# New places for the pre-core and post-core stages in a software pipeline written out by hand

## The chip, the cores and the metric

The kernel runs on one core of a Trainium2 chip. The metric is the device time of one execution in microseconds (us), the median of several runs. A core has five engines that work beside each other, each from a queue of its own and strictly in order: PE (TensorE, matrix products into PSUM banks), DVE (VectorE), ACT (ScalarE), POOL (GpSimd) and SP (SyncE, which only issues DMAs here). They meet through semaphores.

## The reference

There are 16 samples of 512 tokens with 128 channels. Each goes through four residual blocks, each behind a layer normalisation:

```
x = x + block_a(_layernorm(x))     # Mamba block: conv, 16 states, scan over 512 tokens, feed-forward
x = x + experts(_layernorm(x))     # e1: 8 heads, product keys 32 x 32, 8192 experts
x = x + block_b(_layernorm(x))     # gated scan with 16 states, one row each
x = x + experts(_layernorm(x))     # e2: the same expert weights
```

Block a computes for each of 256 inner channels and 16 states `h = exp(delta*A)*h + delta*u*B`, and `y = sum over the states of h*C`. The expert layer forms, for each token and head, two sets of 32 similarities, takes the best key of each, and fetches one of 8192 pairs of rows (`w_down`, `w_up`) by the two keys. The token's result is `gelu(x . w_down) * relu(score) * w_up`, summed over the eight heads.

## The kernel before, in words

The 128 partitions hold channels in the scans and tokens elsewhere; a sample has 4 tiles of 128 tokens. The work of a sample has three phases. The *core* is the scan of block a: for state n, ACT makes the decay `dA` (L1027), PE broadcasts B and C (L759, L768), DVE feeds (L1338), scans (L1354, 128x1024) and reads out (`hp` times C, L1364); for states 1, 3, ..., 13 POOL does the read-out (L1483) from a copy of C that ACT makes (`c_row`, L1044). PE adds the products of all states up in `ysum` (L784), and DVE gates the sum (L1450). *Pre-core* is what comes ahead of it (norm, convolution, silu, the step sizes), *post-core* what follows: the rest of block a, e1, block b, e2.

`run_pipeline` goes through iterations -1 to 19. Iteration i holds the core of sample i, the pre-core of sample i + 1 and the post-core of samples i - 1 to i - 4, so up to six samples are in flight. Iterations 5 to 14 are a hardware loop with two iterations in its body. An iteration is cut into 64 slots, four for each state of the core. Each engine's program goes through the slots in order and issues the stages that `SLOTS` puts there: a post-core slot s means slot s % 64 of iteration (sample + 1 + s // 64). From iteration 15 on, `LAST_SLOTS` replaces the places where it has an entry. A slot is no time: it only sets the order in which an engine meets its stages. What a stage waits for is the same wherever it stands.

An expert layer has these stages, with two halves of two token tiles or four tiles each. PE `sim` (L680) makes the similarities of a tile in one of two PSUM banks; DVE `top` takes the maxima (L1233) and a mask of where they are (L1240). For two tiles, PE `flip` transposes the masks (L691), ACT `flip` copies them (L987), PE `code` turns them to codes (L703), and DVE `index` reads the codes (`bits`, L1249) and makes row numbers (L1258). POOL `fetch` issues eight stages of four indirect gathers (L1468) for the four tiles; its first stage of a half waits for the index and for the previous sample's `sum` to have read the row buffer, and later ones for the landing of the stage two before. DVE `dot` multiplies the rows with the token (L1267, eight for a tile), ACT takes the gelu (L994), DVE `weigh` makes coefficients (L1274), ACT `scale` multiplies the rows (L1006), PE `sum` adds them (L713, L717) and ACT `out` takes the result out (L999).

PE's two shared banks are guarded: `claim` waits until the consumer of the bank's previous content has read it, `fill` notes the next. ACT has to load a table when it changes between groups of functions; `needs` (L934) issues the load where the next function in order asks for another table than the last:

```
if table[0] != name:
    act.preload_act_table_set(name)
    table[0] = name
```

So the number of loads follows from the order on ACT alone. SP issues the loads of x for the residual (`sp_xres`) and the stores of y (`sp_store`).

Of the kernel before, what the change touches and what calls it, by code (L numbers as in the profile page):

```python
# [58 lines left out]
    "pe_turn_x": (PRE, (10,)),  # L59
    "pe_conv": (PRE, (13, 18, 24, 26)),  # L60
    "pe_xproj": (PRE, (35,)),
    "pe_rest": (PRE, (38, 42)),
    "pe_dt": (PRE, (43, 44)),
    "pe_skip": (CORE, (58,)),
    "pe_out": (POST, (0,)),
    "pe_ff1": (POST, (0,)),
    "pe_ff2": (POST, (7,)),
    "pe_ln_a": (POST, (10,)),
    "pe_turn_e1": (POST, (27,)),
# [4 lines left out]
    "pe_turn_b": (POST, (118,)),  # L74
    "pe_xp": (POST, (120,)),
    "pe_gate": (POST, (122,)),
    "pe_y": (POST, (124,)),
    "pe_z": (POST, (143,)),
    "pe_ln_c": (POST, (147,)),
# [6 lines left out]
    "act_rms_x": (PRE, (3,)),  # L86
    "act_keep_x": (PRE, (10,)),
    "act_norm_x": (PRE, (4,)),
    "act_turn_x": (PRE, (6,)),
    "act_conv": (PRE, (14, 19, 24, 28)),  # L90
    "act_silu": (PRE, (30, 63)),
    "act_dbl": (PRE, (34,)),
    "act_soft": (PRE, (42, 47)),
    "act_split": (PRE, (37, 41)),
    "act_exp": (PRE, (55,)),
    "act_ln": (PRE, (56,)),
    "act_out": (POST, (1,)),
    "act_gelu": (POST, (2,)),
    "act_rstd_a": (POST, (5,)),
    "act_rstd_e1": (POST, (17,)),  # L100
    "act_norm_e1": (POST, (24,)),
    "act_turn_e1": (POST, (29,)),
    "act_flip_e1": (POST, (42, 51)),
    "act_gelu_e1": (POST, (64, 81)),
    "act_scale_e1": (POST, (70, 72, 86, 91)),
    "act_out_e1": (POST, (91, 96)),
    "act_rstd_b": (POST, (108,)),
    "act_norm_b": (POST, (120,)),
    "act_turn_b": (POST, (121,)),
    "act_xp": (POST, (125,)),  # L110
    "act_gate": (POST, (125,)),
    "act_tanh": (POST, (128,)),
    "act_rstd_c": (POST, (144,)),
    "act_rstd_e2": (POST, (171,)),
    "act_norm_e2": (POST, (174,)),
    "act_turn_e2": (POST, (177,)),
# [1452 lines left out]
```

## Time and profile before

| what | value |
|---|---|
| time, median of three runs | 1968.15 us (1953.9 to 1971.99) |
| profiled execution | 1957.38 us, span 1955.6 us |
| mean granted clock of PE | 0.938 |
| busy: DVE | 1661.3 us (85%), 4204 instructions |
| busy: PE | 1608.4 us (82%), 6097 matmuls |
| busy: ACT | 1537.7 us (79%), 3276 instructions |
| busy: POOL | 1358.5 us (69%), 1209 instructions |

The shares are means over stages with different limits. The first samples fill the pipeline; the gatings of samples 1 to 14 follow each other in 92 to 109 us; the gating of sample 15, at 1716.20, ends the last core iteration; and from there to 1955.6 the post-core of the last samples runs with no core beside it. A view by windows keeps these stretches apart.

### The profile page before, as it was taken

What the parts mean: (1) busy time and instruction counts of PE and PEld (TensorE: products, weight loads), DVE (VectorE), ACT (ScalarE), POOL (GpSimd) and SP (SyncE); (2) the same over time, 40 slices, a digit from 0 to 9 for tenths busy, and PEclk for the clock granted to TensorE, in tenths of its full rate; (3) what the DMA queues carried; (4) which work ended last, traced back from release to release, by engine and by line L of the source; (5) the groups of instructions that cost most, each with busy time, mean ns of one, the idle gap of its engine ahead of it and who ended that gap; (6) DMA issues with size and microseconds to landing.
All of it is one profiled execution on the core that took longest, in us unless ns stands there. A gap on an engine that the chain in (4) does not pass through costs nothing. (4 is left out here: it accounts for less than half of the span.)

```text
span 1955.6 us, 24773 instructions
## 1 busy us (share of the span) xinstructions
PE 1608.4 (82%) x6097; PEld 887.0 (45%) x6186; DVE 1661.3 (85%) x4204; ACT 1537.7 (79%) x3276; POOL 1358.5 (69%) x1209
## 2 busy tenths in 40 slices
PE   5788788879898988898898989898989986766653
PEld 2333344445454545454454545454545443444332
DVE  3889989899998999999999999999999998844431
ACT  5666778789897979898898989898998975465543
POOL 0234647488877787787778788777778777776665
PEclk8899899999999999999999999999999997997776
DMA  2000212023323223232323232322323232233232
GB/s 60 11 11 27 71 29 70 27 79 86 88 83 93 81 79 96 76 98 81 93 84 90 84 99 79 92 87 67 103 81 95 83 85 83 76 102 98 87 95 83
DMA packets 79901, 151.06 MB, mean 77 GB/s; under 512 B 20584, under 2 KB 46592, under 8 KB 79680
## 3 DMA queue, kind: packets, MB, share of 16 engines
q0 software_dynamic: 49152, 134.28, 24.0%
q1 hardware_dynamic: 29344, 14.65, 2.7%
q8 instruction: 61, 1.00, 0.2%
q14 instruction: 96, 0.79, 0.1%
q10 hardware_dynamic: 1248, 0.34, 0.1%
HBM read 145.01 MB, written 4.19 MB: 76 GB/s over the span
## 5 line engine op out<-in xcount | busy, mean ns | idle before, releaser
L1468 POOL DMA_INDIRECT rows<-in_experts,index x1024 | 981.9, 959 | 357.2 <-issue 288.8
L1354 DVE TENSOR_TENSOR_SCAN hp<-dA,fed_ps 128x1024 f32<-128x1024 f32 x256 | 583.7, 2280 | 7.7 <-issue 2.9
L784 PE MATMUL ysum<-hp,ident 128*128 128x512 f32 x1024 | 487.6, 621 | 4.0 <-DVE hp L1364 3.4
L1483 POOL TENSOR_TENSOR hp<-hp,c_row 128x1024 f32<-128x1024 f32 x112 | 264.8, 2364 | 219.7 <-ACT c_row L1044 178.0
L1027 ACT ACTIVATE dA<-delta,decay 128x511 f32<-128x511 f32 x512 | 334.7, 711 | 17.2 <-issue 15.4
L1338 DVE TENSOR_TENSOR fed_ps<-du,b_ps 128x1024 f32<-128x1024 f32 x256 | 313.7, 1225 | 39.2 <-PE b_ps L759 23.5
L1006 ACT ACTIVATE rows<-rows,coef 128x128 f32<-128x128 f32 x1024 | 311.1, 390 | 13.1 <-DVE coef L1274 13.1
L784 PEld LDWEIGHTS ysum<-hp,ident 128*128 128x128 f32 x1024 | 206.7, 202 | 219.4 <-issue 201.7
L934 ACT ACT_TABLE_LOAD x218 | 279.7, 1283 | 8.8 <-PEq L544 5.0
L717 PE MATMUL bank<-rows,ident 128*128 128x256 f32 x1024 | 251.2, 402 | 32.5 <-ACT rows L1006 32.5
L1267 DVE CUSTOM_DVE_ANT_0 rows<-rows,xn 128x128 f32<-128x128 f32 x1024 | 240.9, 298 | 39.5 <-DMA rows<-in_experts,index 39.1
L717 PEld LDWEIGHTS bank<-rows,ident 128*128 128x128 f32 x1024 | 208.2, 204 | 67.3 <-ACT rows L1006 35.1
L680 PE MATMUL bank<-w_sim,xnT 128*128 128x512 f32 x256 | 151.4, 676 | 46.9 <-DVE mask L1240 32.8
L1364 DVE TENSOR_TENSOR hp<-hp,c_ps 128x1024 f32<-128x1024 f32 x144 | 174.4, 1211 | 13.0 <-remote 12.5
L1233 DVE TENSOR_REDUCE top<-bank 128x16 f32<-128x512 f32 x128 | 86.9, 679 | 43.7 <-PE bank L680 42.7
L810 PE MATMUL bank<-xrT,w_taps 128*128 128x512 f32 x256 | 117.3, 601 | 2.4 <-ACT ucs L1118 1.5
L759 PE MATMUL b_ps<-split,pick 128*128 128x512 bf16 x243 | 97.2, 400 | 21.9 <-DVE fed_ps L1338 11.7
L768 PE MATMUL c_ps<-split,pick 128*128 128x512 bf16 x182 | 73.3, 403 | 38.3 <-DVE hp L1364 30.0
L1240 DVE TENSOR_TENSOR mask<-bank,top 128x512 bf16<-128x512 f32 x128 | 88.6, 692 | 13.0
L999 ACT ACTIVATE x<-bank 128x256 f32<-128x256 f32 x64 | 24.2, 379 | 90.1 <-PE bank L717 89.5
L680 PEld LDWEIGHTS bank<-w_sim,xnT 128*128 128x128 f32 x256 | 43.6, 201 | 113.1 <-DVE mask L1240 63.8
L987 ACT ACTIVATE flip<-bank 128x1024 bf16<-128x1024 bf16 x64 | 65.0, 1015 | 36.3 <-PE bank L691 34.9
(182 smaller groups left out, 2195.4 us busy)
## 6 DMA issues: line engine op xcount, KB each, us to landing
rows<-in_experts,index POOLq DMA_INDIRECT x1024, 2.7
x_in<-in_x SPq DMA_DIRECT2D x16, 256.0 KB, 4.1
x_res<-in_x SPq DMA_DIRECT2D x16, 256.0 KB, 4.7
y<-x SPq DMA_DIRECT2D x16, 256.0 KB, 2.7
rows<-in_taps SPq DMA_DIRECT2D x1, 512.0 KB
rows<-in_wq_t SPq DMA_DIRECT2D x1, 512.0 KB, 5.2
rows<-in_in_proj_t ACTq DMA_DIRECT2D x1, 256.0 KB
rows<-in_key_t SPq DMA_DIRECT2D x1, 128.0 KB, 5.2
```

Source lines behind the costliest of these rows:

```text
L680: nc.tensor.matmul(bank[k][:], e.xnT[:, t * P:(t + 1) * P], w_sim[:], start=True, stop=True).then_inc(e.sim, 1)
L717: mm = nc.tensor.matmul(total, ident[:], e.rows[:, tiles, h, P:2 * P], start=False, stop=(h == HEADS - 1), skip_group_check=True)
L784: mm = nc.tensor.matmul(ysum[:, j, :], ident[:], hp[:, BUFFER[k], j, :], start=(k == SUM_ORDER[0]), stop=(k == SUM_ORDER[-1]))
L934: act.preload_act_table_set(name)
L1006: op = nc.scalar.activation(row, row, ACT.Copy, scale=e.coef[:, t, h:h + 1])
L1027: op = nc.scalar.activation(dA[:, n % NDA, j, 1:T], delta[q][:, j, 1:T], ACT.Exp, scale=decay[:, j, n:n + 1])
L1267: op = nc.vector.tensor_tensor_reduce(row, row, e.xn[r][:, t, :], 1.0, 0.0, ALU.mult, ALU.add, e.dot[:, t, h:h + 1])
L1338: nc.vector.tensor_tensor(fed_ps[:], src[:], b_ps[:].to_broadcast([P, NH, T]), ALU.mult).then_inc(fed, 1)
L1354: nc.vector.tensor_tensor_scan(flat, dA[:, n % NDA, :, :].rearrange("p a b -> p (a b)"), fed_ps[:].rearrange("p a b -> p (a b)"), 0.0, ALU ...
L1364: nc.vector.tensor_tensor(state, state, c_ps[:].to_broadcast([P, NH, T]), ALU.mult).then_inc(read_out, 1)
L1468: pool.indirect_dma_start(e.rows[:, t, h, :], None, A["experts"], bass.IndirectOffsetOnAxis(ap=e.index[:, t, h:h + 1], axis=0)).then_inc(e ...
L1483: pool.tensor_tensor(state, state, c_row[:, k % NCR, :].unsqueeze(1).to_broadcast([P, NH, T]), ALU.mult).then_inc(pool_read, 1)
```

## The change

The numbers in `SLOTS` and `LAST_SLOTS` are new; nothing else is changed. Every stage still issues the same instructions with the same waits and the same buffers. The order in which an engine meets its stages changes on PE, ACT, DVE and POOL; on SP the order is the same. Of the roughly 150 changed entries these are the ones of which the text speaks, and some around them:

```diff
 SLOTS = {
...
-    "pe_sim_e1": (POST, (35, 39, 44, 45)),
-    "pe_flip_e1": (POST, (42, 49)),
-    "pe_code_e1": (POST, (43, 49)),
+    "pe_sim_e1": (POST, (33, 38, 43, 48)),
+    "pe_flip_e1": (POST, (40, 49)),
+    "pe_code_e1": (POST, (42, 52)),
...
-    "pe_turn_e2": (POST, (175,)),
-    "pe_sim_e2": (POST, (176, 178, 185, 186)),
-    "pe_flip_e2": (POST, (180, 192)),
-    "pe_code_e2": (POST, (184, 193)),
-    "pe_sum_e2": (POST, (236, 251)),
+    "pe_turn_e2": (POST, (176,)),
+    "pe_sim_e2": (POST, (179, 180, 183, 185)),
+    "pe_flip_e2": (POST, (181, 190)),
+    "pe_code_e2": (POST, (182, 197)),
+    "pe_sum_e2": (POST, (240, 251)),
...
-    "act_silu": (PRE, (30, 63)),
+    "act_silu": (PRE, (30, 59)),
...
-    "act_flip_e2": (POST, (184, 192)),
-    "act_gelu_e2": (POST, (221, 239)),
-    "act_scale_e2": (POST, (224, 228, 241, 252)),
+    "act_flip_e2": (POST, (187, 192)),
+    "act_gelu_e2": (POST, (220, 246)),
+    "act_scale_e2": (POST, (228, 237, 252, 253)),
...
-    "dve_top_e1": (POST, (38, 40, 45, 48)),
-    "dve_index_e1": (POST, (42, 53)),
-    "dve_dot_e1": (POST, (54, 63, 75, 78)),
-    "dve_weigh_e1": (POST, (66, 82)),
+    "dve_top_e1": (POST, (36, 39, 47, 48)),
+    "dve_index_e1": (POST, (40, 52)),
+    "dve_dot_e1": (POST, (60, 62, 67, 76)),
+    "dve_weigh_e1": (POST, (68, 81)),
...
-    "dve_top_e2": (POST, (177, 180, 184, 185)),
-    "dve_index_e2": (POST, (183, 198)),
-    "dve_dot_e2": (POST, (210, 219, 228, 237)),
-    "dve_weigh_e2": (POST, (224, 239)),
+    "dve_top_e2": (POST, (178, 180, 183, 184)),
+    "dve_index_e2": (POST, (181, 198)),
+    "dve_dot_e2": (POST, (212, 220, 228, 242)),
+    "dve_weigh_e2": (POST, (224, 245)),
-    "pool_delta": (PRE, (59,)),
-    "pool_x1": (POST, (4,)),
-    "pool_x3": (POST, (120,)),
-    "pool_fetch_e1": (POST, (39, 42, 44, 53, 61, 62, 66, 70)),
-    "pool_fetch_e2": (POST, (192, 201, 205, 209, 214, 219, 223, 228)),
-    "sp_xres": (POST, (14,)),
-    "sp_store": (POST, (234,)),
+    "pool_delta": (PRE, (55,)),
+    "pool_x1": (POST, (5,)),
+    "pool_x3": (POST, (121,)),
+    "pool_fetch_e1": (POST, (39, 44, 46, 53, 55, 56, 57, 58)),
+    "pool_fetch_e2": (POST, (187, 198, 207, 211, 218, 220, 225, 228)),
+    "sp_xres": (POST, (35,)),
+    "sp_store": (POST, (251,)),
 LAST_SLOTS = {
...
-    "pe_sim_e2": (POST, (164, 171, 178, 180)),
+    "pe_sim_e2": (POST, (171, 171, 184, 190)),
...
-    "pe_sum_e2": (POST, (240, 244)),
+    "pe_sum_e2": (POST, (243, 253)),
...
-    "act_gelu_e2": (POST, (221, 243)),
-    "act_scale_e2": (POST, (232, 235, 243, 244)),
+    "act_gelu_e2": (POST, (227, 242)),
+    "act_scale_e2": (POST, (231, 235, 247, 250)),
...
-    "dve_top_e2": (POST, (168, 175, 179, 180)),
-    "dve_index_e2": (POST, (175, 203)),
-    "dve_dot_e2": (POST, (218, 220, 242, 243)),
+    "dve_top_e2": (POST, (171, 174, 190, 191)),
+    "dve_index_e2": (POST, (177, 196)),
+    "dve_dot_e2": (POST, (212, 222, 241, 247)),
...
-    "pool_fetch_e1": (POST, (35, 37, 47, 47, 48, 49, 53, 62)),
-    "pool_fetch_e2": (POST, (176, 177, 204, 210, 212, 219, 220, 227)),
+    "pool_fetch_e1": (POST, (27, 31, 32, 40, 50, 52, 55, 56)),
+    "pool_fetch_e2": (POST, (187, 196, 200, 207, 210, 212, 218, 238)),
```

On DVE a loop iteration had, from slot 48 on:

```
scan 12, top_e1.3, feed 13, top_e2.0, mul 12, scan 13, top_e2.1, feed 14, index_e1.1, dot_e1.0,
index_e2.0, scan 14, top_e2.2, feed 15, top_e2.3, mul 14, scan 15, mul 15, scan_b, dot_e1.1
```

and has with the change:

```
scan 12, top_e1.3, feed 13, mul 12, dot_e2.3, top_e2.0, scan 13, top_e2.1, index_e1.1, feed 14,
index_e2.0, weigh_e2.1, top_e2.2, scan 14, top_e2.3, feed 15, mul 14, scan 15, dot_e1.0, mul 15,
dot_e1.1, scan_b
```

where `mul` is the read-out and the number behind the point is the tile or half. On PE, ahead of the flips of e2's first half, stood `sum_e2.0, sim_e1.3, turn_e2, sums of 12, sim_e2.0, flip_e1.1, code_e1.1, sim_e2.1, sums of 13`, and now `turn_e2, sim_e1.3, sum_e2.0, flip_e1.1, sim_e2.0, sums of 13, sim_e2.1, code_e1.1`.

## Rows read from the trace of the kernel before

**Rows 1.** Windows: length, busy PE, PEld, DVE, ACT, POOL (count), PEclk, DMA, GB/s.

```profile
950.70:1057.50 106.80, 94.66 (x381) 53.00 (x388) 101.75 (x262) 97.76 (x207) 84.82 (x76) 1.00 0.31 87
...
1591.50:1717.40 125.90, 93.12 (x351) 52.23 (x354) 107.46 (x248) 74.19 (x181) 93.54 (x88) 0.88 0.29 85
...
1870.00:1955.60 85.60, 36.85 (x149) 24.74 (x147) 24.54 (x166) 33.75 (x96) 47.69 (x51) 0.72 0.30 86
```

**Rows 2.** Waits of DVE, 629 to 1483 us (eight iterations): total, times, longest.

```profile
DVE hp L1364 <- remote: 9.1, 8, 1.1
DVE top L1233 <- PE bank L680: 4.2, 4, 1.1
...
DVE fed_ps L1338 <- issue: 0.2, 1, 0.2
```

**Rows 3.** Timeline of DVE in iteration 10: start, duration, instruction.

```profile
1139.52 0.69 DVE L1240 TENSOR_TENSOR mask<-bank,top 128x512 bf16<-128x512 f32 x1
1140.12 1.22 DVE L1338 TENSOR_TENSOR fed_ps<-du,b_ps 128x1024 f32<-128x1024 f32 x1
1141.25 0.18 DVE L1249 TENSOR_SCALAR bits<-bank 128x32 int32<-128x32 int32 x1
...
1141.96 0.29 DVE L1267 CUSTOM_DVE_ANT_0 rows<-rows,xn 128x128 f32<-128x128 f32 x1
...
1143.66 0.19 DVE L1249 TENSOR_SCALAR bits<-bank 128x32 int32<-128x32 int32 x1
...
1144.20 2.29 DVE L1354 TENSOR_TENSOR_SCAN hp<-dA,fed_ps 128x1024 f32<-128x1024 f32 x1
```

**Rows 4.** Timeline, last samples: a mask and the bits that wait for it.

```profile
1888.39 0.69 DVE L1240 TENSOR_TENSOR mask<-bank,top 128x512 bf16<-128x512 f32 x1
...
1891.83 0.19 DVE L1249 TENSOR_SCALAR bits<-bank 128x32 int32<-128x32 int32 x1 [2.75 <-PE bank L703]
```

**Rows 5.** Timeline near 1750 us: a mask and the next maximum.

```profile
1749.17 0.69 DVE L1240 TENSOR_TENSOR mask<-bank,top 128x512 bf16<-128x512 f32 x1
...
1751.07 0.69 DVE L1233 TENSOR_REDUCE top<-bank 128x16 f32<-128x512 f32 x1 [1.22 <-PE bank L680]
```

**Rows 6.** Timeline of PE in iteration 10.

```profile
1137.39 3.60 PE L784 MATMUL ysum<-hp,ident 128*128 128x512 f32 x8
```

**Rows 7.** Groups by line: count, busy, mean ns, idle before.

```profile
L934 ACT ACT_TABLE_LOAD x218 | 279.7, 1283 | 8.8 <-PEq L544 5.0
```

**Rows 8.** Timeline of ACT about a table load.

```profile
1829.97 1.28 ACT L934 ACT_TABLE_LOAD   x1
1831.27 0.30 ACT L939 ACTIVATE lnB<-mvB,eps 128x4 f32<-128x4 f32 x1
```

**Rows 9.** Timeline of DVE, last core iteration: first scan and gating.

```profile
1591.46 2.27 DVE L1354 TENSOR_TENSOR_SCAN hp<-dA,fed_ps 128x1024 f32<-128x1024 f32 x1
...
1716.20 1.23 DVE L1450 TENSOR_TENSOR ucs<-ysum,ucs 128x1024 f32<-128x1024 f32 x1 [2.60 <-PE ysum L784]
```

**Rows 10.** Waits of ACT, 1591 to 1717 us.

```profile
ACT act L994 <- DVE dot L1267: 17.9, 4, 13.7
```

**Rows 11.** Timeline of POOL, 1717 to 1940 us: the gathers that waited, and the last.

```profile
1756.76 0.94 POOL L1468 DMA_INDIRECT rows<-in_experts,index  x1 [4.99 <-DVE index L1258]
...
1782.26 0.94 POOL L1468 DMA_INDIRECT rows<-in_experts,index  x1 [5.80 <-issue]
...
1850.74 0.94 POOL L1468 DMA_INDIRECT rows<-in_experts,index  x1 [7.47 <-PE bank L717]
...
1899.14 0.94 POOL L1468 DMA_INDIRECT rows<-in_experts,index  x1 [6.33 <-PE bank L717]
...
1938.00 0.95 POOL L1468 DMA_INDIRECT rows<-in_experts,index  x1 [0.30 <-issue]
```

**Rows 12.** Timeline of SP at the end.

```profile
1952.90 0.37 SPq L640 DMA_DIRECT2D y<-x  x1
```

**Rows 13.** Waits of DVE, 45 to 215 us.

```profile
DVE fed_ps L1338 <- PE b_ps L759: 9.4, 5, 3.7
```

More of the change, by code:

```diff
@@ L58 @@
 SLOTS = {
[L59 to L63, printed above, removed]
+    "pe_turn_x": (PRE, (8,)),
+    "pe_conv": (PRE, (10, 17, 24, 25)),
+    "pe_xproj": (PRE, (33,)),
+    "pe_rest": (PRE, (37, 40)),
+    "pe_dt": (PRE, (41, 43)),
     "pe_skip": (CORE, (58,)),
     "pe_out": (POST, (0,)),
-    "pe_ff1": (POST, (0,)),
+    "pe_ff1": (POST, (3,)),
     "pe_ff2": (POST, (7,)),
-    "pe_ln_a": (POST, (10,)),
@@ L97 @@
+    "act_conv": (PRE, (13, 21, 25, 28)),
+    "act_silu": (PRE, (30, 59)),
+    "act_dbl": (PRE, (36,)),
+    "act_soft": (PRE, (39, 41)),
+    "act_split": (PRE, (37, 38)),
+    "act_exp": (PRE, (48,)),
+    "act_ln": (PRE, (50,)),
     "act_out": (POST, (1,)),
-    "act_gelu": (POST, (2,)),
-    "act_rstd_a": (POST, (5,)),
+    "act_gelu": (POST, (1,)),
+    "act_rstd_a": (POST, (4,)),
     "act_rstd_e1": (POST, (17,)),
-    "act_norm_e1": (POST, (24,)),
-    "act_turn_e1": (POST, (29,)),
-    "act_flip_e1": (POST, (42, 51)),
@@ L104 @@
[L104 to L109, printed above, removed]
+    "act_norm_e1": (POST, (23,)),
+    "act_turn_e1": (POST, (28,)),
+    "act_flip_e1": (POST, (39, 54)),
+    "act_gelu_e1": (POST, (64, 79)),
+    "act_scale_e1": (POST, (71, 71, 86, 89)),
+    "act_out_e1": (POST, (90, 98)),
+    "act_rstd_b": (POST, (101,)),
+    "act_norm_b": (POST, (119,)),
@@ L170 @@
-    "pe_sum_e2": (POST, (240, 244)),
+    "pe_out": (POST, (0,)),
+    "pe_ff1": (POST, (0,)),
+    "pe_ff2": (POST, (8,)),
+    "pe_ln_a": (POST, (15,)),
+    "pe_turn_e1": (POST, (26,)),
+    "pe_sim_e1": (POST, (26, 28, 33, 33)),
+    "pe_flip_e1": (POST, (30, 40)),
+    "pe_code_e1": (POST, (31, 40)),
+    "pe_sum_e1": (POST, (81, 85)),
+    "pe_turn_b": (POST, (108,)),
+    "pe_xp": (POST, (112,)),
+    "pe_gate": (POST, (112,)),
+    "pe_y": (POST, (117,)),
+    "pe_z": (POST, (132,)),
+    "pe_ln_c": (POST, (136,)),
@@ L171 @@
+    "pe_turn_e2": (POST, (160,)),
+    "pe_sim_e2": (POST, (171, 171, 184, 190)),
+    "pe_flip_e2": (POST, (174, 191)),
+    "pe_code_e2": (POST, (174, 199)),
+    "pe_sum_e2": (POST, (243, 253)),
     "act_out": (POST, (3,)),
     "act_gelu": (POST, (3,)),
[L173 to L174 removed]
+    "act_rstd_a": (POST, (9,)),
+    "act_rstd_e1": (POST, (19,)),
     "act_norm_e1": (POST, (24,)),
[L176 to L177 removed]
@@ L205 @@
[L205 to L215 removed]
+    "act_turn_e1": (POST, (25,)),
@@ new lines @@
+    "act_flip_e1": (POST, (30, 42)),
+    "act_gelu_e1": (POST, (51, 76)),
+    "act_scale_e1": (POST, (72, 76, 77, 77)),
+    "act_out_e1": (POST, (83, 88)),
+    "act_rstd_b": (POST, (90,)),
+    "act_norm_b": (POST, (99,)),
+    "act_turn_b": (POST, (111,)),
+    "act_xp": (POST, (112,)),
+    "act_gate": (POST, (112,)),
+    "act_tanh": (POST, (126,)),
+    "act_rstd_c": (POST, (136,)),
+    "act_rstd_e2": (POST, (140,)),
+    "act_norm_e2": (POST, (150,)),
+    "act_turn_e2": (POST, (159,)),
@@ new lines @@
+    "act_flip_e2": (POST, (173, 194)),
+    "act_gelu_e2": (POST, (227, 242)),
+    "act_scale_e2": (POST, (231, 235, 247, 250)),
+    "act_out_e2": (POST, (242, 252)),
+    "dve_x1": (POST, (15,)),
+    "dve_stats_e1": (POST, (16,)),
+    "dve_shift_e1": (POST, (20,)),
+    "dve_top_e1": (POST, (26, 29, 32, 34)),
+    "dve_index_e1": (POST, (31, 44)),
+    "dve_dot_e1": (POST, (41, 53, 67, 71)),
+    "dve_weigh_e1": (POST, (66, 76)),
+    "dve_stats_b": (POST, (92,)),
+    "dve_shift_b": (POST, (93,)),
```

107 lines of the change are left out of this document (29 added, 78 removed).

## The prediction

> **What bounds the kernel now.** I read the windows by stage first, because the kernel has three different regimes [rows 1]. In the loop, from one gating of the scan's sum to the next, DVE is busy 101.75 of 106.80 us, ACT 97.8, PE 94.7, POOL 84.8, at the full granted clock: DVE is the bound. In the last core iteration DVE is busy 107.5 of 125.9 us, and in the last stretch 24.5 of 85.6 while the clock is down to 0.72. The reader should then see, in the table of waits over eight loop iterations, how little DVE has left to win [rows 2]: 9.1 us for the read-out of state 15, 4.2 us for the similarities of the key search, and so on down to 0.2 us. Its eight kinds of wait come to 22.6 us in eight iterations, 2.8 us each. A new order cannot shorten DVE's work; in the loop it can win at most these 2.8 us an iteration, while what it can lose has no such lid. For the last core iteration and what follows, the timelines of DVE and POOL are read, where one sees who waits for whom; they stand with their parts below.
>
> **The change, part by part.** No instruction is added or removed, and no wait or buffer. What changes is the order in which each engine's queue holds its stages. I wrote out both orders for each engine and iteration and asked, for each wait, which work now stands between the producer and the consumer.
>
> *Loop, the e2 search (loss).* Before, DVE has between the second mask of e2 (ends 1140.21) and the first index of e2 (1143.66) a feed of 1.22 us, an index of 0.7 us and a dot stage of 1.7 us, so 3.5 us of cover [rows 3]. Behind a mask the chain PE flip, ACT flip, PE code takes 2.75 us until DVE can read its bits; this row is at a reduced clock, so at full clock I take 2.4 as the lower end [rows 4]. Afterwards the dot stage has left this place; feed and index are all the cover there is, 1.75 us from the mask's end to the index's (1140.21 to 1141.96). The stall is 2.4 to 2.75 less 1.75, so 0.65 to 1.0. On ACT two table loads and the second silu now stand ahead of this flip too; they may add half a microsecond or hide behind the PE's stages. I take 0.9, bounds 0.4 to 1.5.
>
> *Loop, third similarity of e2 (loss).* From a mask to the next maximum on the same bank the trace shows 1.22 us of waiting through PE's matmul pair [rows 5]. Before, a scan of 2.29 us stands there and hides it [rows 3]; afterwards only a weigh stage does, one short instruction. Because the two banks alternate, part may hide: I take 1.1, bounds 0.7 to 1.3.
>
> *Loop, two smaller losses.* The first index of e1 has one scan (2.29) ahead of it in place of feed, read-out and statistics: against the same chain 0.3, bounds 0 to 0.6. The second similarity of e2 is now behind the summing of state 12 and 13 on PE, which takes 3.60 us [rows 6], while DVE does a dot stage, a maximum with its mask and a scan: 0.5, bounds 0 to 1. The loss comes to 0.9 + 1.1 + 0.3 + 0.5 = 2.8 us an iteration, bounds 1.1 to 4.4.
>
> *Loop, gains.* The first dot stage of e1 (1.7 us) moves to between scan 15 and the read-out of state 15, where DVE waits 9.1/8 = 1.14 us [rows 2]; that wait is covered whole. The fourth similarity of e1 gets a scan for cover, which should end the similarity waits, 4.2/8 = 0.53 [rows 2]; smaller ones give 0.2. Gain 1.9, and it is nearly the lid. Net +0.95 us an iteration, bounds -0.3 to +2.3. The full post-core work stands in iterations 3 to 14, so twelve times: +11 us, bounds -4 to +28.
>
> *Loop, other engines.* Counted from ACT's order, the table loads fall from the 218 of the trace to 205, one less in each loop iteration. At 1.283 us that frees 16.7 us of ACT [rows 7], but ACT is not the bound, so I cost it at nothing; its cover is ACT's own 9 us of slack in each iteration [rows 1]. POOL now issues the last two e1 stages and the first e2 stage at the end of an iteration and spills 13 to 15 us into the next; the first POOL read-out then comes some 3 to 5 us later by the same hand walk, still before PE sums its state, and POOL has 22 us of slack [rows 1]. The loading of the residual moves 21 slots later and the store 17; the queue of SP holds them in the same order and both land long before their readers, so nothing.
>
> At one place a row and a rule part. When ACT changes its table, the load takes 1.28 us and the next ACTIVATE starts 0.02 us after it [rows 8]. The Trainium skill, "ScalarE: Activation LUTs", section "What ACT_TABLE_LOAD costs", gives 1283 ns for the load and another 1380 ns for a drain, some 2.66 us a switch. By that the thirteen saved loads would be worth 35 us of ACT, still off DVE's path; the trace agrees on the load and shows no drain here.
>
> *Last core iteration (gain).* From its first scan (1591.46) to its gating (1716.20) it takes 125 us [rows 9], some 18 longer than a loop iteration; ACT waits 13.7 us at once for a dot stage [rows 10], which waits for its fetched rows. POOL here does the fetches of two samples ahead of time, and the new places issue e1 of sample 14 from slot 27 in place of 35, and defer three e2 stages. Walking the order by hand with the durations of these rows puts the gating 112 to 122 us after the first scan; I take 117, so -8, bounds -13 to 0. Against it: the gating now stands behind the last two similarity stages of e2 of sample 12 and a sum of sample 11 on PE, and its wait of 2.60 us [rows 9] grows to some 8 us, which is in the 117.
>
> *Tail (gain).* After the gating POOL does little but issue row gathers, at a pitch of 0.95 + 0.30 = 1.25 us, so a stage of four is 5.0 us; it has four waits: 4.99 (for the index of sample 15), 5.80, 7.47 and 6.33 us, the last three before the first e2 stage of samples 13, 14 and 15 [rows 11]. In the new order the last e2 stage of sample 12 and the first two of sample 13 are issued among and behind e1 of sample 15: the 5.80 goes with its place. Behind the 7.47 stood six stages, 30 us, since the last fetch of e1, so the chain it waited for is 37.5 us long; now eight stages and a short addition stand there, some 41 us, and it vanishes too: -13.3. One more stage comes after the index of sample 15: +5.0. That index comes about 1.3 us later, and the last output has one gelu more ahead of it, +0.25. If the 6.33 us wait keeps its length, -7; if it ends when it did, 0. I take -4, with the upper bound at +2. From the last gather (1938.95) to the store (1952.90) 14 us pass [rows 11, 12]; that stays.
>
> *Head (unknown).* In the first iterations DVE waits 9.4 us in five waits for B's broadcast [rows 13]. Some places ahead of it become earlier, one later; no row prices that, so a few of these 9.4 us either way: -2, bounds -5 to +3.
>
> **Sum.** +11 - 8 - 4 - 2 = -3 us. The profiled execution took 1957.4 us, 10.8 under the median of the three runs: it should become 1954, and the median 1965.
>
> **Rivals.** (A) The covers suffice, faster: if PE and ACT are ahead of DVE at these places, the losses of the loop shrink to 0.2 and the gain of 1.9 stays: 12 x -1.7 = -20; with -8, -4 and -2 that is -34, so 1934. For it: PE and ACT are idle 12 and 9 us in a loop iteration, so they can be early. Against it: the chain behind a mask begins with DVE's own mask, and no idle time elsewhere shortens it.
> (B) The e2 search becomes DVE's bound, slower: PE's run of turn, sum, similarity, summing, similarity comes late as one, and each of DVE's four e2 similarities then waits. The upper end of the loop, 2.3 x 12 = +28, with nothing won in the last core iteration, gives 1996. It decides from more than 1 us of waiting ahead of the second e2 similarity in each iteration, or a gating more than 125 us after the first scan of sample 15. For it: the stages of e2 now stand back to back. Against it: the read-out wait is surely covered.
> (C) Only the order in a saturated queue changes, and every wait that goes comes back elsewhere: 1968.
> (D) The two table loads that now stand ahead of the first e2 flip each cost twice their 1.28 us, because ACT empties before a load: 2 x 1.28 more a loop iteration, 12 x 2.6 = +31, so 1996. The row with 0.02 us after a load speaks against it. It is the rule of the Trainium skill's page "ScalarE: Activation LUTs", section "What ACT_TABLE_LOAD costs".
>
> **Chances.** My forecast 0.36, (A) 0.30, (B) 0.22, (C) 0.08, (D) 0.04. One per cent, 20 us, is about what a measurement of this kernel can tell from no change, since its own three runs lie 18 us apart. Faster by over 1%: 0.30 from (A). Within: 0.36 + 0.08 = 0.44. Slower: 0.22 + 0.04 = 0.26. My forecast by itself spans 1949 to 1985 (its bounds added as squares, -16 and +20); the range reaches to (A) and to (B) and leaves out a tenth beyond either: 1930 to 1998.
>
> **What would show it.** In the changed kernel's loop: waits of the bits for PE's code of about 0.9 + 0.3 us an iteration, and of the maximum for the similarity of about 1.5; no wait of the read-out of state 15; a period near 107.7 us. 205 table loads. The gating of sample 15 near 117 us after its first scan. One wait in place of three between POOL's e2 stages in the tail, and the end some 235 us after that gating. I am wrong if the loop's period falls under 106 (A) or exceeds 109 (B, D), or if the last gating comes later than before.

## The result, and the profile after

The changed kernel takes 2008.83 us (median, 2007.79 to 2009.21) where the kernel before took 1969.47: ratio 1.0222, 95% interval 1.0179 to 1.0266. It is slower by 2.2%, where 0.2% faster was forecast, and it lies above the stated range. Its executions differ by 1.4 us; those of before by 18.

The profiled execution has a span of 2007.0 us, 51.4 more than before. Cut at the gatings, as in [rows 1, 9]:

| stretch | before, us | after, us | difference | forecast |
|---|---|---|---|---|
| start to gating of sample 2 | 311.1 | 310.9 | -0.2 | -2 |
| iterations 3 to 14 | 1279.2 | 1341.9 | +62.7 | +11 |
| last core iteration | 125.9 | 121.4 | -4.5 | -8 |
| gating of sample 15 to end | 239.4 | 232.8 | -6.6 | -4 |

So the whole error lies in the loop, whose period rose from 106.7 to 112.6 us. The windows of the changed kernel (one loop iteration, the last core iteration, the tail; columns as in [rows 1]):

```profile
1089.60:1202.30 112.70, 98.21 (x380) 56.34 (x386) 107.02 (x261) 94.41 (x204) 85.46 (x76) 0.94 0.29 83
1652.80:1774.20 121.40, 91.40 (x345) 50.67 (x349) 105.71 (x247) 68.55 (x163) 85.34 (x78) 0.90 0.27 78
1774.20:2007.00 232.80, 138.66 (x574) 90.72 (x574) 86.75 (x514) 122.33 (x332) 158.13 (x166) 0.76 0.34 98
```

The reader should see that DVE is busy 107.0 us in an iteration of the loop, for the work that took it 101.75 [rows 1]; the counts, 261 and 262, differ only by where the windows are cut. The same work has become longer. Its waits, over eight iterations as in [rows 2], grew too, but less:

```profile
DVE top L1233 <- PE bank L680: 19.1, 25, 1.3
DVE s L1367 <- ACT rr L941: 8.8, 4, 2.4
DVE bits L1249 <- PE bank L703: 5.7, 8, 0.7
DVE fed_ps L1338 <- PE b_ps L759: 1.1, 3, 0.4
```

The wait for the read-out of state 15 is gone, as forecast. Which instructions are longer is read from the groups by line, over the same eight iterations (busy, mean ns, idle before). First the kernel before:

```profile
L1267 DVE CUSTOM_DVE_ANT_0 rows<-rows,xn 128x128 f32<-128x128 f32 x512 | 114.6, 286 | 0.2
...
L1437 DVE TENSOR_TENSOR_SCAN gates<-gates 16x512 f32<-16x512 f32 x8 | 9.7, 1212 | 0.3
...
L1258 DVE TENSOR_SCALAR index<-code 128x16 uint32<-128x16 f32 x32 | 5.8, 180 | 1.1
```

and the changed kernel:

```profile
L1267 DVE CUSTOM_DVE_ANT_0 rows<-rows,xn 128x128 f32<-128x128 f32 x512 | 113.9, 285 | 0.5 <-DMA rows<-in_experts,index 0.2
...
L1258 DVE TENSOR_SCALAR index<-code 128x16 uint32<-128x16 f32 x32 | 29.5, 922 | 1.1
L1437 DVE TENSOR_TENSOR_SCAN gates<-gates 16x512 f32<-16x512 f32 x8 | 21.9, 2734 | 0.3
```

Two groups out of some thirty hold the rise: the last instruction of the index stage, +23.7 us, and the scan of block b, +12.2 us, together 4.5 us an iteration. Neither is a long instruction by itself. What POOL does at such a moment is seen when the two timelines are laid beside each other. The index stage of iteration 10 on DVE:

```profile
1102.35 0.17 DVE L1254 SCALAR_TENSOR_TENSOR code<-bits 128x16 f32<-128x16 int32 x1
1102.56 4.07 DVE L1258 TENSOR_SCALAR index<-code 128x16 uint32<-128x16 f32 x1
1106.54 2.27 DVE L1354 TENSOR_TENSOR_SCAN hp<-dA,fed_ps 128x1024 f32<-128x1024 f32 x1
```

and POOL over the same stretch:

```profile
1102.06 0.95 POOL L1468 DMA_INDIRECT rows<-in_experts,index  x1 [0.30 <-issue]
1103.03 2.35 POOL L1483 TENSOR_TENSOR hp<-hp,c_row 128x1024 f32<-128x1024 f32 x1
1105.32 1.26 POOL L1489 TENSOR_TENSOR x_res<-x_res,ln_b 128x512 f32<-128x512 f32 x1
```

An instruction of 0.17 us began under a gather, was then held through POOL's read-out of state 1 and the addition right behind it, and ended 0.05 us after that addition (1106.63 against 1106.58). POOL lost nothing: 2.35 and 1.26 us are its ordinary times. The scan of block b, on DVE in iteration 9:

```profile
1085.64 2.78 DVE L1437 TENSOR_TENSOR_SCAN gates<-gates 16x512 f32<-16x512 f32 x1
...
1088.46 1.23 DVE L1338 TENSOR_TENSOR fed_ps<-du,b_ps 128x1024 f32<-128x1024 f32 x1
```

with POOL's addition for block b under it, and behind that a gather that is itself 0.75 us longer than its 0.95:

```profile
1086.07 1.27 POOL L1494 TENSOR_TENSOR xnb<-x,beta 128x512 f32<-128x512 f32 x1
1087.50 1.70 POOL L1468 DMA_INDIRECT rows<-in_experts,index  x1 [0.16 <-issue]
```

In the kernel before, the same scan began under gathers alone in each loop iteration and took 1.21 us. I call it a meeting when a DVE instruction is lengthened in this way. Summed over the whole execution as the excess of each instruction over its group's usual time, meetings hold 17.6 us in the kernel before, all but about 1 us of it in iterations 1 to 3 and 15, and 60.4 us in the changed kernel.

The other predicted rows: 205 table loads at 1283 ns, as counted. The first index of sample 15 reached POOL 41.4 us after the gating, 0.8 us later than before, where 1.3 was forecast. Of the three later waits in the tail one went and two stayed, shorter (rows to be held against [rows 11, 12]):

```profile
1815.57 0.95 POOL L1468 DMA_INDIRECT rows<-in_experts,index  x1 [2.60 <-DVE index L1258]
...
1906.60 0.94 POOL L1468 DMA_INDIRECT rows<-in_experts,index  x1 [4.55 <-issue]
...
1950.17 0.94 POOL L1468 DMA_INDIRECT rows<-in_experts,index  x1 [2.69 <-issue]
```

### The profile page after: what moved, and what is told of

Read it like the earlier page. It is cut to its first block and busy times, and to the rows that moved or that the text cites. A ratio compares the mean times of both kernels' runs of the same rounds, so it can differ in the third digit from the quotient of the medians.

```text
span 2007.0 us, 24736 instructions
## 1 busy us (share of the span) xinstructions
PE 1645.5 (82%) x6097; PEld 919.5 (46%) x6186; DVE 1701.2 (85%) x4204; ACT 1520.9 (76%) x3263; POOL 1364.7 (68%) x1209
## 5 line engine op out<-in xcount | busy, mean ns | idle before, releaser
L1354 DVE TENSOR_TENSOR_SCAN hp<-dA,fed_ps 128x1024 f32<-128x1024 f32 x256 | 582.6, 2276 | 1.7
L1027 ACT ACTIVATE dA<-delta,decay 128x511 f32<-128x511 f32 x512 | 332.7, 711 | 23.7 <-issue 15.3
L1338 DVE TENSOR_TENSOR fed_ps<-du,b_ps 128x1024 f32<-128x1024 f32 x256 | 313.5, 1225 | 26.8 <-PE b_ps L759 16.7
L934 ACT ACT_TABLE_LOAD x205 | 263.0, 1283 | 8.6 <-PEq L544 5.0
L1267 DVE CUSTOM_DVE_ANT_0 rows<-rows,xn 128x128 f32<-128x128 f32 x1024 | 241.5, 298 | 27.0 <-DMA rows<-in_experts,index 26.5
L680 PE MATMUL bank<-w_sim,xnT 128*128 128x512 f32 x256 | 160.2, 711 | 38.4 <-DVE mask L1240 16.6
L759 PE MATMUL b_ps<-split,pick 128*128 128x512 bf16 x243 | 102.4, 421 | 29.8 <-DVE fed_ps L1338 23.0
L1044 ACT ACTIVATE c_row<-c_ps 128x512 f32<-128x512 f32 x112 | 65.6, 586 | 51.9 <-PE c_ps L768 39.3
```

The source lines that it names most:

```text
L680: nc.tensor.matmul(bank[k][:], e.xnT[:, t * P:(t + 1) * P], w_sim[:], start=True, stop=True).then_inc(e.sim, 1)
L1027: op = nc.scalar.activation(dA[:, n % NDA, j, 1:T], delta[q][:, j, 1:T], ACT.Exp, scale=decay[:, j, n:n + 1])
L1267: op = nc.vector.tensor_tensor_reduce(row, row, e.xn[r][:, t, :], 1.0, 0.0, ALU.mult, ALU.add, e.dot[:, t, h:h + 1])
L1338: nc.vector.tensor_tensor(fed_ps[:], src[:], b_ps[:].to_broadcast([P, NH, T]), ALU.mult).then_inc(fed, 1)
L1354: nc.vector.tensor_tensor_scan(flat, dA[:, n % NDA, :, :].rearrange("p a b -> p (a b)"), fed_ps[:].rearrange("p a b -> p (a b)"), 0.0, ALU ...
```

## The experiments

The theory (P): in the new order POOL's instructions on tensors run at the same time as DVE instructions that take two operands from SBUF, or one in a fast form, and hold them; the order costs by these meetings. The first rival (Q): the loss sits in waits for PE and ACT, and the long records are a symptom.

The Trainium skill, "SBUF — State Buffer", section "Who interferes with whom", says that DVE and GpSimd share a second pair of SBUF ports under an exclusive lock, and that a DVE instruction with two SBUF inputs, or one like `tensor_scalar` in a two-port mode, is blocked by a GpSimd instruction that reads SBUF for its whole length, while one that takes at most one input from SBUF in a plain mode is not. The runs agree: in the changed kernel and in those around it, lengthened were the dot (L1267), the score, code, coefficient, offset and index instructions (L1251, L1254, L1274, L1217, L1258) and the scan of block b, all with SBUF operands alone, while the 256 scans of the states, one operand of which lies in PSUM, kept a mean of 2276 ns (2280 before). In all the kept traces one scan of a state is long, 3.90 us in run 11, and its record lies inside that of an index instruction that was held until the same moment. In which mode the index instruction ran, no trace shows. I had not weighed this rule before the run.

For each run, the period, DVE's busy time and the rest are read from the windows between the gatings of samples 5 and 13, divided by eight; they stand in one table at the end of this section.

**1. The addition for block b, one place earlier** (on the changed kernel).

```diff
-    "pool_x3": (POST, (121,)),
+    "pool_x3": (POST, (118,)),
```

> The changed kernel with one place moved: POOL's addition for block b (x3) ahead of the step sizes (slot 118 in place of 121), so that it no longer stands beside DVE's scan of block b. Theory P (POOL and DVE shut each other out of SBUF while both read two operands there): that scan falls from 2.78 to 1.21 us in each loop iteration, 12 x 1.57 = 19 us, so about 1990 us. Rival Q (the loss is in the waits for PE and ACT that the new order makes): the scan's length is a symptom of something else, and the time stays at 2009 within 5 us.

Measured: 1994.68 us (1991.42 to 2008.46), ratio to before 1.0181 [1.011, 1.0253]. The scan of block b is short in all sixteen samples:

```profile
L1437 DVE TENSOR_TENSOR_SCAN gates<-gates x16: 1211/1212/1214, 309.5 to 1901.5; 16x512 f32<-16x512 f32 x16
```

```profile
L1437 DVE TENSOR_TENSOR_SCAN gates<-gates x16: 1212/2778/2800, 308.6 to 1901.9; 16x512 f32<-16x512 f32 x16
```

The first row is this run, the second the changed kernel (shortest, median and longest in ns). 14 us of the 19 came back in the median, but beside this run the kernel before took 1957.13 us and not 1969.47; by the ratios (1.0222 and 1.0181, whose intervals overlap) it is some 8 us. The profiled execution was the slowest (2008.46), with a loop as long as that of the changed kernel: in it 13 dot stages met POOL's read-outs, 30.1 us, where three had. There the gain was taken back by a meeting elsewhere.

**2. The codes in PSUM.** The instruction, its place and its waits stay; it reads another memory.

```diff
-                nc.vector.scalar_tensor_tensor(out=e.code[:, tiles, :], in0=e.bits[:, tiles, 0:HEADS],
+                code = bank[k][:, 2 * HALF * GR:2 * HALF * GR + HALF * HEADS].rearrange("p (t g) -> p t g", t=HALF)
+                nc.vector.scalar_tensor_tensor(out=code, in0=e.bits[:, tiles, 0:HEADS],
...
-                nc.vector.tensor_scalar(e.index[:, tiles, :], e.code[:, tiles, :], 0.5,
+                nc.vector.tensor_scalar(e.index[:, tiles, :], code, 0.5,
```

> The changed kernel with the codes of the index stage written to PSUM (free columns of the bank from which the bits came) in place of SBUF, so that the last instruction of the stage reads PSUM. Order, waits and counts are those of the changed kernel. Theory P: all 64 of these instructions take 0.2 us or less, where 12 took 0.4 to 4.1 us; 28 us of DVE's time vanish, 24 to 28 of them on the path, so about 1983 us. Rival Q: the long ones are a wait for POOL to be done with the old index, or a record of something else, and stay: 2009 us.

Measured: 2009.88 us, ratio 1.0246 [1.0169, 1.0323]. All 64 are short, and the time has not moved:

```profile
L1259 DVE TENSOR_SCALAR index<-bank x64: 173/174/176, 177.5 to 1970.9; 128x16 uint32<-128x16 f32 x64
```

The rival's reading of the record falls: with its operand in PSUM the instruction is never held. But the expected 26 us did not come. In this run 12 dot stages meet POOL's read-outs, 27.5 us in all, in place of three with 7.3. Where the index no longer waits, DVE comes to its next stages earlier, and meets POOL there.

**3. Both edits.**

> Both edits at once. Theory P: the two gains add up to 43 to 47 us, the loop's period falls from 112.6 to about 108 us, and the time is near 1964 us, close to the kernel before. Rival Q: 2009 us, and the period stays over 112.

Measured: 1989.43 us, ratio 1.0163 [1.0093, 1.0233]; period 110.9. Less than half of what P expected. In the loop the dots are now what meets: in every other iteration the dot behind the scan of state 7 meets the read-out of state 7, and the one behind the scan of state 9 that of state 9, 2.1 and 2.5 us each.

**4. POOL's old entries in the changed kernel** (`pool_delta` 55 to 59, `pool_x1` 5 to 4, `pool_x3` 121 to 120, and both fetches as before).

> The changed kernel with POOL's five entries of the first table as before (the last table, and PE, ACT, DVE and SP, as changed). Theory P: POOL's multiplication of state 1 and its additions no longer meet the index stage and the scan of block b, both long forms vanish and the time is near 1964 us, if the old places of the gathers make no new wait for rows with the new places of the dot stages. Rival Q: PE, ACT and DVE hold the loss, POOL's order is nearly free, and the time stays over 2000 us.

Measured: 2042.98 us, ratio 1.0426 [1.0352, 1.0499]. P is missed; Q's "over 2000" is met, but not its ground, since POOL's order was not nearly free: this order of POOL costs 2% more than the changed one. POOL's old order was harmless only beside DVE's old order. Here 75 us of meetings stand in the trace: dots with read-outs 26.8, coefficients with read-outs 17.3, index and score stages most of the rest.

**5. POOL's new entries in the kernel before**, the reverse.

> The kernel before with POOL's five entries of the first table as changed (the reverse of the run that gave the changed kernel POOL's old entries and took 2043 us). Theory P: what counts is the phase of POOL's read-outs and additions against DVE's stages with two operands in SBUF, which neither order has by itself: POOL now spills into the next iteration, its multiplication of state 1 meets the index stage in slot 6, and the time rises by 15 to 45 us. Rival Q: POOL has 20 us of slack in an iteration, and its order costs nothing in the queue that bounds the loop: within 4 us of before.

Measured: 2030.01 us, ratio 1.0354 [1.0299, 1.0409], 70 us more than the kernel before took beside it, where P expected 15 to 45. The sharpest of the one-sided runs, since DVE, PE and ACT keep their old order here. DVE's busy time rises by 6.5 us an iteration and the rest by 0.2. The dots (mean 286 ns before) hold the rise, and the list of waits begins as that of before does [rows 2]; two views of this run, groups by line and waits, 700 to 1600 us:

```profile
L1267 DVE CUSTOM_DVE_ANT_0 rows<-rows,xn 128x128 f32<-128x128 f32 x504 | 165.6, 390 | 0.5
```

```profile
DVE hp L1364 <- PE c_ps L768: 9.1, 8, 1.1
DVE s L1367 <- ACT rr L941: 4.0, 3, 1.8
```

The index stage, which P had named as the one to be met, was not (176 ns); the dots were. P's mechanism holds, its place was wrong again.

**6. One dot of the kernel before, moved onto a read-out on purpose.**

```diff
-    "dve_dot_e1": (POST, (54, 63, 75, 78)),
+    "dve_dot_e1": (POST, (54, 63, 75, 80)),
```

> The kernel before with one number changed: the last dot stage of e1 stands behind the scan of state 4 in place of ahead of it (slot 78 to 80). Nothing else moves. In the trace of before POOL multiplies state 3 from 4.8 to 7.1 us after the end of the scan of state 3; DVE would begin this dot at 4.7 us. Theory P: the dot stage, 1.8 us by itself, is held until POOL is through, 2.3 us more in each loop iteration, 12 x 2.3 = 28 us, near 1985 us against 1957 before. Rival Q: moving 1.8 us of work past one scan is free in a queue that never idles: within 4 us of before.

Measured: 2003.98 us (1986.5 to 2006.34), ratio 1.0178 [1.0095, 1.0262]. One number changed costs 1.8%. In the profiled execution, the fastest of the five, the dot meets the read-out of state 3 in each iteration from 2 to 14 and is longer by 2.2 to 2.7 us, where 2.3 was worked out. DVE and POOL in iteration 12:

```profile
1317.80 2.93 DVE L1267 CUSTOM_DVE_ANT_0 rows<-rows,xn 128x128 f32<-128x128 f32 x1
```

```profile
1318.22 2.35 POOL L1483 TENSOR_TENSOR hp<-hp,c_row 128x1024 f32<-128x1024 f32 x1
```

A second meeting came with it, the coefficients of e2 with the read-out of state 7, 1.0 us in each iteration from 5 to 14. This is the only meeting placed by a hand calculation that came where it was calculated and close to its size; rival Q, that the place is free, falls.

**7. No meetings by dodging them**: both edits of run 3, and four dots one slot earlier.

```diff
-    "dve_dot_e1": (POST, (60, 62, 67, 76)),
+    "dve_dot_e1": (POST, (60, 62, 67, 75)),
...
-    "dve_dot_e2": (POST, (212, 220, 228, 242)),
+    "dve_dot_e2": (POST, (211, 219, 227, 242)),
```

> Both edits of the run before (codes in PSUM, the addition for block b earlier), and four dot stages of DVE one slot earlier (e1 76 to 75, e2 212, 220, 228 to 211, 219, 227), so that each stands ahead of the scan that releases a POOL read-out and not directly behind it. Theory P: what was left of the meetings, 33 us of dot stages that met the read-outs of states 7 and 9, goes; the loop's period falls by about 2 to 3 us an iteration, and the time is near 1960 us. Rival R (the meetings are only moved about: whatever DVE does while POOL reads out, it loses the same): other dots or feeds become longer instead and the time stays within 8 us of 1989.

Measured: 1983.73 us (1977.89 to 1988.62), ratio 1.0074 [1.0037, 1.0111]. The meetings are gone (7.6 us in the whole execution) and DVE's busy time is that of before, 102.0 us, but the period is still 110.9 us. What DVE won it now waits, in the eight iterations of the table:

```profile
DVE top L1233 <- PE bank L680: 26.7, 24, 2.1
DVE rows L1268 <- DMA rows<-in_experts,index: 10.1, 8, 1.6
DVE bits L1249 <- PE bank L703: 9.4, 16, 1.3
```

The second row is the edit's own: a dot that was moved ahead of a scan now waits 1.3 us for its gathered rows. R's number is met (5 us from 1989), but not its ground, since the meetings did not only move about; the time P expected did not come. By the ratios (1.0163 in run 3, 1.0074 here) something was gained, which the loop of the profiled execution does not show.

**8. The third maximum of e2 behind the scan again**, on top of run 7.

```diff
-    "dve_top_e2": (POST, (178, 180, 183, 184)),
+    "dve_top_e2": (POST, (178, 180, 184, 185)),
```

> The same, and the third maximum of e2 behind the scan of state 14 as before, in place of ahead of it (slot 183 to 184). By the term of the prediction the wait for that similarity costs 1.1 us an iteration: some 13 us less than the run without this edit, near 1947 us. Rival: the wait moves to the fourth maximum, which then has less behind it, and the time is the same within 5 us.

Measured: 1985.87 us, ratio 1.0102 [1.001, 1.0193]: no gain. The wait before that maximum is gone from the timeline, but the waits for similarities over eight iterations fell only from 26.7 to 23.4 us: those before the fourth maxima of e1 and e2 grew. The rival is right.

**9 and 10. The search of e2 as before**, on top of run 7: ten entries of the first table (PE turn, sim, flip, code, sum; ACT norm, turn, flip; DVE top, index), then with the first dot of e1 back at slot 54.

> The run without meetings (codes in PSUM, the addition for block b earlier, four dot stages one slot earlier), with the ten entries of the search of e2 in the first table as before (PE turn, sim, flip, code, sum; ACT norm, turn, flip; DVE top, index). Theory W (with the meetings gone the loop is held by the waits that the new search order makes, as the prediction's terms say): the waits for the second and third similarity, 1.04 + 1.64 us an iteration, go; the first index keeps about 0.7 since its dot stage is still away. Period from 110.2 to about 107.5 us, 12 x 2.7 = 32 us less: near 1952 us. Rival V (the waits are only where a loop that PE and ACT hold shows itself, PE at the lower clock): they come back elsewhere, and the time is within 8 us of 1984.

> The same, with the first dot stage of e1 back between the feed and the first index of e2 (slot 60 to 54). Theory W: the 0.7 us of that index goes and the 1.14 us wait for the read-out of state 15 comes back: 5 us slower than the run without this, near 1957 us. Rival: the covered wait of state 15 is paid anyway, as the gating waits for the sum behind it; then this is 8 us faster.

Measured: 2087.54 us, ratio 1.067 [1.0602, 1.0738], and 2128.48 us, ratio 1.0897 [1.0815, 1.0979]. Both expectations failed, for a reason of the mixture: on PE the fourth similarity of e1 now stood behind the turn and the first similarity of e2, while on DVE its maximum stood ahead of e2's. Waits of run 9, 700 to 1600 us:

```profile
DVE top L1233 <- PE bank L680: 69.3, 19, 7.8
DVE bits L1249 <- PE bank L703: 20.2, 21, 2.3
```

They tell nothing on the rest of the loss, but they do tell how large a wait becomes when two engines' orders don't fit.

**11. The last table alone** (first table as before).

> The first table as before, the last table as changed. By the prediction the last core iteration gives 8 us and the tail 4: 12 us faster than before. In the trace of the changed kernel they gave 4.5 and 6.6: 11 us. Theory P says the same unless the last core iteration makes new meetings (before has five of them there, 7.8 us). Rival: the gains belong to the first table's order, which leaves POOL less to do when the last core begins: no change within 4 us.

Measured: 1965.02 us, ratio 0.9998 [0.9949, 1.0047]. The interval ends at 0.5% faster, 10 us, so the expected 12 us did not come; between 10 us and nothing the run does not decide, and its trace, of its slowest execution, is no basis for the last core iteration. The tail there is 232.9 us, as in every run with this last table (231 to 237 us), against 239.4 before and 241.1 in run 5; so the shorter tail goes with the last table.

**12 and 13. POOL's work cut short, nothing moved.** Read-outs over 32 of 512 tokens, additions over 8 of 128 channels, in the changed kernel and in the one before.

```diff
-                        state = hp[:, BUFFER[n], :, :]
+                        state = hp[:, BUFFER[n], :, 0:32]
```

> The changed kernel with POOL's work cut short where it meets DVE: the read-outs of the seven POOL states touch 32 of 512 tokens, and the two additions 8 of 128 channels (so states and residuals are left unfinished there). Order, waits and all other instructions as changed. Theory P: without anything to meet, DVE's long instructions are as short as in before; the 4.4 us an iteration go, and what is left over before is the 1.8 us of waits and knock-on: period near 108.5 us, about 1968 us. Theory W+P (what is left when meetings are gone is a loop held by waits at about 110 us, as in the run that dodged them): meetings vanish and the period is still 110 us, about 1985 us.

> The kernel before with the same work left out on POOL, as control. In the trace of before no loop iteration has a meeting, and DVE waits for POOL nowhere. Theory P: the period stays at 106.6 us and only the 17 us of meetings in the first and last iterations can go: 1945 to 1957 us. Rival: shorter POOL work by itself helps PE's sums and all that follows: under 1935 us; then the gain of the run beside it is not the meetings' alone.

Measured: 2013.25 us, ratio 1.027 [1.0206, 1.0334], and 1944.15 us, ratio 0.9911 [0.9874, 0.9948]. The control did as expected, its loop unmoved (106.7 us over iterations 3 to 14). The changed kernel did not: POOL's two step-size instructions had been left whole, and the first, 2.35 us, was now met by nine code and three score instructions, 32.7 us.

**14 and 15. The step sizes cut short too** (32 of 512 tokens).

```diff
-                        pool.tensor_tensor(delta[r][:], delta[r][:], du[r][:], ALU.add).then_inc(delta_done, 1)
+                        pool.tensor_tensor(delta[r][:, :, 0:32], delta[r][:, :, 0:32], du[r][:, :, 0:32], ALU.add).then_inc(delta_done, 1)
```

> As the changed kernel with short POOL work, and the two step-size instructions of POOL cut short too (32 of 512 tokens; the rest of the step sizes stays unfinished): in the run before this one they took the place of the others, and nine index stages met them. Now no POOL instruction with tensors is longer than 0.4 us. Theory P: the period falls from 112 to about 108.5 us, that is the 106.7 of before and the waits' 1.8; near 1965 us. Theory W+P: the waits alone hold the loop at about 110 us; near 1985 us. Rival W only: it stays at 112, 2010 us, and meetings were never what the loop waited for.

> The control: the kernel before with the same work left out on POOL. Theory P and W+P: the loop has no meetings to lose, its period stays at 106.6 us, and the time at about 1944 us, as with the step sizes left whole. Rival: the step sizes are ready 4 us earlier, the next core starts earlier, and the period falls by 1 us or more.

Measured: 1968.15 us (1959.91 to 1970.58), ratio 1.0007 [0.998, 1.0033], and 1938.35 us, ratio 0.9872 [0.9822, 0.9922]. The time is that of theory P (1965 us; its rivals had 1985 and 2010). The period, 108.9 us over iterations 3 to 14 and 109.3 over the eight of the table, lies between P's 108.5 and the 110 of W+P. In the control the rival's faster period did not come (106.9 and 107.2 us). Windows between the same two gatings, the changed kernel whole, then run 14, then the control:

```profile
639.50:1540.00 900.50, 792.72 (x3026) 453.51 (x3074) 848.46 (x2081) 759.90 (x1632) 684.09 (x601) 0.93 0.29 83
```

```profile
634.50:1509.00 874.50, 787.59 (x3025) 437.86 (x3072) 815.93 (x2082) 759.48 (x1632) 521.40 (x601) 0.95 0.29 85
```

```profile
619.20:1476.40 857.20, 766.47 (x3025) 426.68 (x3072) 812.95 (x2082) 769.49 (x1641) 521.54 (x601) 0.98 0.30 87
```

DVE's busy time falls from 848.5 to 815.9 us with not one DVE instruction changed or moved; the scan of block b takes 1.21 us in all sixteen samples and no index instruction more than 0.42. The kernels that bear on the loop, per iteration of these eight:

| kernel | period, us | DVE busy | the rest |
|---|---|---|---|
| before | 106.7 | 101.7 | 5.0 |
| changed | 112.6 | 106.1 | 6.5 |
| 1, addition earlier | 112.6 | 105.5 | 7.1 |
| 2, codes in PSUM | 112.7 | 105.2 | 7.5 |
| 3, both | 110.9 | 103.8 | 7.0 |
| 4, POOL as before | 114.6 | 107.2 | 7.4 |
| 5, before with POOL's new order | 113.4 | 108.2 | 5.2 |
| 6, before with one dot moved | 109.7 | 105.0 | 4.7 |
| 7, dodged | 110.9 | 102.0 | 8.9 |
| 14, changed, POOL short | 109.3 | 102.0 | 7.3 |
| 15, before, POOL short | 107.2 | 101.6 | 5.5 |

## Why the prediction was wrong

**The loop's bound was read rightly, its consequence wrongly.** DVE is the bound, as the windows said. The step that failed is the sentence that a new order cannot shorten DVE's work, out of which I took that it cannot lengthen it, and with it the one on POOL: it "spills 13 to 15 us into the next" iteration, "still before PE sums its state, and POOL has 22 us of slack", so nothing. The read-out of state 1 did come later, and no one waited for its result. But DVE's index stage stood at that place, and POOL's additions now stood beside the scan of block b. An engine with slack was costed at nothing because nobody waits for it by a semaphore; a held instruction shows no wait. It shows as busy time, 4.4 us an iteration.

**What it costs.** Between the changed kernel and run 14 lie 2008.83 - 1968.15 = 40.7 us (ratios to before 1.0222 and 1.0007), with nothing moved: this is shown to be POOL's length under DVE's instructions. In the profiled executions the twelve loop iterations fall from 1341.9 to 1307.0 us, 34.9 of the 62.7 lost there, while the control's loop does not fall (1279.2 and 1282.2). Over the whole execution the share is smaller, since the kernel before loses its own meetings outside the loop: in the control the stretch to the gating of sample 2 falls from 311.1 to 302.0 us and the last core iteration from 125.9 to 116.5. With POOL short in both, the new order is still 29.8 us slower (1968.15 against 1938.35, 1.5%).

**The waits were named, but in sum mis-sized.** What is left in the loop without meetings is 1307.0 - 1282.2 = 24.8 us, 2.1 an iteration, against the forecast +0.95 with bounds -0.3 to +2.3. (The bounds of the terms, added plainly, give -0.8 to +2.5.) Nearly all of it is in waits: those of DVE come to 43.1 us in eight iterations of run 14 and to 27.1 in the control, 2.0 an iteration apart. By their places in the changed kernel's timeline: the first index of e2 waits 0.71 us in every iteration (forecast 0.9); the third similarity 1.16 (1.1); the first index of e1 0.14 (0.3); the second similarity 1.04, where I took 0.5 and had 1 as its bound. Iteration 10 on PE, in one view:

```profile
1173.00 3.60 PE L784 MATMUL ysum<-hp,ident 128*128 128x512 f32 x8
1176.43 1.02 PE L680 MATMUL bank<-w_sim,xnT 128*128 128x512 f32 x2
...
1182.11 1.12 PE L680 MATMUL bank<-w_sim,xnT 128*128 128x512 f32 x2 [0.70 <-DVE index L1258]
```

The summing ends as DVE's scan ends (1176.45), so it is hidden and the whole pair of the second similarity is waited for. The pair of the third starts, by the releaser that the row names, behind the index stage of DVE, and not behind a mask as in my term: that its size was right is luck. The gain at state 15 is whole (1.14 gone); that at the fourth similarity of e1 is 0.4 of 0.53 in the changed kernel and none in run 14, where that wait is 0.9 to 1.3 us in each of the eight iterations. There DVE also waits 0.5 us an iteration before the feed of state 12, for B's broadcast, which no term had. A new wait of 2.2 us stands before the norm's shift in every other iteration (8.8 us in the waits above); in run 14 it is 3.1 us in eight iterations, so most of it followed from the held scan.

**Last core iteration and tail.** -4.5 for -8 (the gating came 120.2 us after the first scan, not 117), and -6.6 for -4. The wait of 8 us that I had put before the gating stands one stage ahead of it, 6.17 us before the last maximum. With POOL short, where neither order has meetings to speak of, the new one gains 1.2 us here (116.5 to 115.3) and 5.3 in the tail (238.4 to 233.1). In the tail the wait of 5.80 went; the one of 7.47, which I let vanish, is still 4.55, and the one of 6.33 became 2.69.

**The rivals.** (B) had the sign, and 2.3 us of waits an iteration as its price; its point, more than 1 us before the second similarity, is met (1.04). In the loop of the changed kernel it is the smaller part, 24.8 of 62.7 us. (A) and (C) are out. (D) is out: 205 loads, and ACT is not waited for more than before, save for the shift.

**What stays open.** Why removing meetings by moving stages (runs 1 to 3, 7) gave back so much less than removing them by length (run 14) is shown only in part: each time other stages met, or waited for gathered rows and similarities. How much of the 24.8 us is the clock of PE was not tried by itself, and the traces do not separate it. In the changed loop its mean granted clock is 0.93 against 0.99 (0.95 in run 14), so part of the time at the lower level of 1.2 GHz. The control, one order and one load, has iterations of both kinds; two of them, then one of run 14:

```profile
835.00:940.10 105.10, 94.25 (x379) 52.87 (x384) 101.41 (x262) 95.02 (x204) 65.18 (x75) 1.00 0.30 88
1049.30:1158.50 109.20, 98.97 (x379) 54.23 (x384) 101.91 (x261) 95.08 (x205) 65.24 (x76) 0.95 0.30 85
```

```profile
1072.00:1180.80 108.80, 97.61 (x380) 53.72 (x386) 102.19 (x261) 94.71 (x205) 65.95 (x77) 0.97 0.30 87
```

Of the control's eight iterations the five at the full clock take 105.0 to 106.8 us and the three partly at the lower level 109.0 to 109.2; in run 14 all eight are partly at the lower level and take 108.7 to 110.1. The wait for the second similarity is not the clock's: the pair takes 1.02 us, and the summing ahead of it the 3.60 that it has at the full clock [rows 6].

## What to carry to other kernels

Before an engine with slack is moved for nothing, lay its instructions on tensors beside those of the engine that bounds the loop: GpSimd and VectorE can hold each other without any semaphore, and the trace then shows longer instructions, not waits; compare the mean time of each line between two traces. In a saturated loop such meetings are a matter of phase: most edits moved them to another stage, so a place is only good together with the places of the other engine, and an order drawn from the durations of single stages does not know them. What does not move is an operand: the index instruction, once it read PSUM in place of SBUF, took 0.18 us or less in all 64 places of each of the six runs that had it. And once all of GpSimd's work on tensors was short, the meetings were nearly gone with no stage moved (run 14); while one long instruction was left, DVE met that one (run 12).

## What the runs showed of the hardware that I had not expected

- A DVE instruction can be held by two POOL instructions in a row: 0.17 us became 4.07 when the read-out (2.35) was followed at once by the addition (1.26). In every other iteration the same instruction began 0.1 us after the read-out instead of 0.5 us before it, and came free at the read-out's end, after 2.25 us, though the same addition followed.
- Between instructions on tensors the one held was DVE's, even when its record begins first: the dot of run 6 began at 1317.80, POOL's read-out at 1318.22, and the dot ended at 1320.73. The Trainium skill, "SBUF — State Buffer", section "Who interferes with whom", says that whoever issues first gets the shared ports; by the recorded starts that is not what happens here, though whether a record begins where the instruction is issued is not shown. In the three cases shown, POOL was in the middle of a gather when DVE's record begins; whether that decides was not tried.
- A gather on POOL can be held in its turn: the one that begins under the scan of block b ended 0.76 to 0.78 us after that scan in the changed kernel, and took up to 1.87 us in place of 0.95.
- The changed kernel's times lie within 1.4 us, those of before within 18. With all of POOL's work short, four executions of before lie within 7.3 (1934.43 to 1941.74); with its step sizes left whole (run 13), ten lie within 19. What makes the scatter was not tried.
